# The input of a state-space scan copied to PSUM by ScalarE and multiplied there in place, behind the scan; negated maxima written to PSUM

## The reference

```python
# selective scan, D_INNER = 256 channels, 16 states each
def step(ht, inp):
    x_t, dt_t, B_t, C_t = inp
    dA = jnp.exp(dt_t[..., None] * A)
    dB = dt_t[..., None] * B_t[:, None, :]
    ht = dA * ht + dB * x_t[..., None]
    y_t = jnp.sum(ht * C_t[:, None, :], axis=-1)
    return (ht, y_t)
...
# cross-attention, 16 heads of 8
score = jnp.einsum('bhqd,bhkd->bhqk', qh, kh) / jnp.sqrt(jnp.float32(n_d))
attn = jax.nn.softmax(score, axis=-1)
```

## Time and profile before

| | |
|---|---|
| median of 3 runs | 883.94 us (882.31 to 884.08) |
| span of the profiled execution, which is the only time that the profile gives for it | 889.5 us |
| busy over the span: PE, DVE, ACT, POOL | 81%, 80%, 60%, 72% |
| rounds of the scan | from 27 to 623 us |

### The profile page before, as it was taken

How to read it: one execution, slowest core, us unless ns; L and a number is a source line. 1 busy time by engine, 2 the same in 40 slices (tenths; PEclk the granted TensorE clock), 3 DMA queues, 4 the chain that set the end, 5 groups by cost and what they waited for, 6 DMA issues and landing times. The chain is left out here.

```text
span 889.5 us, 12694 instructions
## 1 busy us (share of the span) xinstructions
PE 721.8 (81%) x3977; PEld 491.0 (55%) x3977; DVE 715.8 (80%) x1060; ACT 531.9 (60%) x1272; POOL 639.2 (72%) x481
## 2 busy tenths in 40 slices
PE   6577578888888889888878888847888998899992
PEld 3343344554445455455535545524565787799982
DVE  4789999999999999999999999999435245455782
ACT  4777569669768877876976795681243342233230
POOL 1278899678989889889998988997422445645552
PEclk9788779999999999899999999987899999999997
DMA  4545575274464646347425533960643346675952
GB/s 99 192 149 146 182 266 192 82 251 145 158 178 155 192 121 203 122 135 211 157 109 184 172 120 107 280 203 25 190 129 105 109 158 196 223 253 168 368 183 76
DMA packets 83917, 148.91 MB, mean 167 GB/s; under 512 B 11201, under 2 KB 56143, under 8 KB 83850
## 3 DMA queue, kind: packets, MB, share of 16 engines
q1 hardware_dynamic: 78858, 139.55, 49.3%
q0 software_dynamic: 4992, 8.54, 2.8%
HBM read 115.34 MB, written 39.27 MB: 174 GB/s over the span
## 5 line engine op out<-in xcount | busy, mean ns | idle before, releaser
L1451 POOL TENSOR_TENSOR prod<-hst,BC 128x1024 f32<-128x1024 f32 x128 | 301.4, 2362 | 62.7 <-DVE hst L1663 49.6
L1663 DVE TENSOR_TENSOR_SCAN hst<-dA,Rp 128x1024 f32<-128x1024 f32 x128 | 292.2, 2283 | 6.4
L1188 ACT ACTIVATE dA<-dtm,Aneg 128x255 f32<-128x255 f32 x512 | 214.8, 496 | 66.0 <-DVE hst L1663 64.1
L1571 POOL DMA_INDIRECT y2d<-prod,back x92 | 91.7, 997 | 125.5 <-DVE prod L1964 103.8
L1456 POOL TENSOR_TENSOR prod<-prod 128x512 f32<-128x512 f32 x128 | 163.6, 1288 | 2.4
L1654 DVE TENSOR_TENSOR Rp<-BC,Rp 128x1024 f32<-128x1024 f32 x128 | 157.0, 1226 | 7.8 <-DMA BC<-bcd 0.6
L638 PE MATMUL Y<-prod,ident 128*128 128x256 f32 x512 | 139.2, 405 | 22.8 <-POOL prod L1456 18.0
L638 PEld LDWEIGHTS Y<-prod,ident 128*128 128x128 f32 x512 | 99.1, 201 | 57.9 <-POOL prod L1456 22.5
L638 PE MATMUL Mb<-hpad,winT 128*128 128x512 f32 (+1 forms) x176 | 82.5, 617 | 15.1 <-ACT xh L1137 13.6
L638 PEld LDWEIGHTS Rp<-BC,xh 128*128 128x128 f32 x736 | 89.1, 192 | 4.8 <-issue 2.6
L638 PE MATMUL Rp<-BC,xh 128*128 128x128 f32 x736 | 89.9, 275 | 0.6 <-DVE prod L1964 0.6
(11 more groups left out here) (254 smaller groups left out, 1215.9 us busy)
## 6 DMA issues: line engine op xcount, KB each, us to landing
BC<-bcd SPq DMA_DIRECT2D x63, 1024.0 KB, 5.4
BC<-recs SPq DMA_DIRECT2D x46, 578.0 KB
xsd<-blank SPq DMA_DIRECT2D x18, 1056.0 KB, 12.4
dtm<-xsd SPq DMA_DIRECT2D x46, 132.0 KB
recs<-in_L_ffn_W SPq DMA_DIRECT2D x16, 256.0 KB
xin<-in_x SPq DMA_DIRECT2D x8, 256.0 KB, 5.8
x2d<-x2o SPq DMA_DIRECT2D x8, 256.0 KB, 5.6
E<-x2d SPq DMA_DIRECT2D x4, 512.0 KB
```

Of the source, the lines that this page charges most:

```text
L1188: m = A(dA[:, k % RING, i, 1:SEQ], dtm[:, r % 2, d, b * SEQ + 1:(b + 1) * SEQ], ACT.Exp, scale=Aneg[:, d, c * NC + i:c * NC + i + 1])
L1451: TT(prod[:, k % RING, :, :], hst[:, k % RING, :, :], BC[:, (k // 2) % BCR, 1, :, :], ALU.mult).then_inc(s_pd, 1)
L1571: pool.indirect_dma_start(out=y2d[:, :], out_offset=bass.IndirectOffsetOnAxis(ap=at, axis=0), in_=yr[:, j % YR, i, :], in_offset=None, bou ...
L1663: v.tensor_tensor_scan(hst[:, k % RING].rearrange("p n s -> p (n s)"), dA[:, k % RING].rearrange("p n s -> p (n s)"), U.rearrange("p n s - ...
```

## The change

ScalarE gets a new function `copy_xh`, which copies `xh` of one sequence into `DTX`; it stands in ScalarE's code behind the decays that it computes in steps 7 and 15, and once ahead of the first decays. `steps_x` waits for that copy and multiplies `DTX` by `dtm` in place, so that one of its inputs is in PSUM. It moves from ahead of the scan of steps 7 and 15 to behind it. The reduction `least` and the product `normed` move with it. `split_max` writes the negated maxima to PSUM (up to round 6; in round 7 to an SBUF tile) and splits them from there, with one instruction more.

```diff
+            def copy_xh(r, b):
+
+                if r or b:
+                    act.wait_ge(s_u, r * STEPS + b * (STEPS // 2))
+                    act.wait_ge(Aa.sem, Aa.at("xh1", r))
+                else:
+                    act.wait_ge(Ha.sem, Ha.at("xh1", 0))
+                A(DTX, xh[:, r % 2, :, b * SEQ:(b + 1) * SEQ], ACT.Copy).then_inc(s_xc, 1)
...
             first_half()
+            copy_xh(0, 0)
...
                 g = r * STEPS + k + 3
                 if g < ROUNDS * STEPS:
                     decays(*divmod(g, STEPS))
+                if k == 7:
+                    copy_xh(r, 1)
+                if k == 15 and r + 1 < ROUNDS:
+                    copy_xh(r + 1, 0)
                 slot(r, k)
...
-                if r or b:
-                    v.wait_ge(s_u, r * STEPS + b * (STEPS // 2))
+                v.wait_ge(s_xc, r * NB + b + 1)
                 half = slice(b * SEQ, (b + 1) * SEQ)
-                v.tensor_tensor(DTX[:, :, :], dtm[:, r % 2, :, half], xh[:, r % 2, :, half], ALU.mult).then_inc(s_dx, 1)
+                v.tensor_tensor(DTX[:, :, :], dtm[:, r % 2, :, half], DTX[:, :, :], ALU.mult).then_inc(s_dx, 1)
...
-                v.tensor_scalar(nm[:, :, 0, 0:HEADS], mx[:, :, :], -1.0, None, ALU.mult).then_inc(Tv.sem, 1)
+                v.tensor_scalar(part, mx[:, :, :], -1.0, None, ALU.mult).then_inc(Tv.sem, 1)
                 v.wait_ge(Tv.sem, Tv.at("ma", r))
-                v.scalar_tensor_tensor(part, mx[:, :, :], -1.0, nm[:, :, 0, 0:HEADS], ALU.mult, ALU.subtract).then_inc(Tv.sem, 1)
+                v.tensor_copy(nm[:, :, 0, 0:HEADS], part).then_inc(Tv.sem, 1)
                 v.wait_ge(Tv.sem, Tv.at("mb", r))
+                v.tensor_tensor(part, part, nm[:, :, 0, 0:HEADS], ALU.subtract).then_inc(Tv.sem, 1)
+                v.wait_ge(Tv.sem, Tv.at("mc", r))
                 v.tensor_copy(nm[:, :, 1, 0:HEADS], part).then_inc(Tv.sem, 1)
-                v.wait_ge(Tv.sem, Tv.at("mc", r))
+                v.wait_ge(Tv.sem, Tv.at("md", r))
                 v.tensor_tensor(nm[:, :, 2, 0:HEADS], part, nm[:, :, 1, 0:HEADS], ALU.subtract).then_inc(Tv.sem, 1)
```

```diff
+                if k == 7:
+                    steps_x(r, 1)
+                    if tail:
+                        least(r - 2)
+                if nxt and k == 15:
+                    steps_x(r + 1, 0)
+                if ln and k == 15:
+                    normed(r + 2)
```

More of the change, by code:

```diff
@@ L301, in decoder @@
         s_bc = [sem(f"s_bc{i}") for i in range(BCR)]
+        s_xc = sem("s_xc")
         s_dx = sem("s_dx")
@@ L313, in decoder @@
         Ta = Marks(sem("Ta"), "KT V sq ln rs q m e00 e01 e10 e11 ld rd x2")
-        Tv = Marks(sem("Tv"), "xq " + " ".join(f"mx{i}a mx{i}b" for i in range(NB * QT)) + " ma mb mc me n")
+        Tv = Marks(sem("Tv"), "xq " + " ".join(f"mx{i}a mx{i}b" for i in range(NB * QT)) + " ma mb mc md me n")
         s_kb = sem("s_kb")
@@ L1772, in middle @@
                         logits(r - 2)
-                    if k == 8:
-                        least(r - 2)
                 if k == 11 and r < ROUNDS:
@@ L1780, in middle @@
                     maxima(r - 1, 2)
[L1781 to L1786, removed]
             def slot(r, k):
```

## The result

The changed kernel takes 932.44 us (927.45 to 933.87, 4 runs) against 883.12 (880.61 to 884.08, 4 runs) of the kernel before on the same chip: a ratio of 1.0523, with a 95% interval of 1.0482 to 1.0563. By the medians it is slower by 49.3 us; 49.0 were forecast. By the ratio, taken at 883.1 us, the loss is 46.2 us (42.6 to 49.7). The kernel before is not steady enough to tell the two apart: beside the first four experiments its median was 886.55 us, and against that the loss would be 45.9.

The account below looks back on a forecast made before the run. VectorE bounds the rounds, the engine that the others wait for. The terms 63.4 - 1.7 - 7.7 - 4.7 give +49.3 us, +49.0 at the median's scale: 883.9 + 49.0 = 932.9, so 933 us; 8 in 10 for 921 to 947.

Parts of the forecast that it names:

- The copy of step 7: Rounds 1 to 7: VectorE's dt*x waits for ScalarE's copy, queued behind slot 6, delaying step 8; +63.4 us together.
- the forecast's 8 to 13 and about 6: Expected VectorE idle time in us ahead of the second dt*x: 8 to 13 in most rounds, about 6 in round 7.
- Step 15: Copy for the first sequence is hidden by the scan; 1.1 us saved at each of 7 places, -7.7 us.
- A cover: At step 15 the copy was to end 0.5 us before the product could start.
- The split: Split of the maxima, 6 rounds: first instruction, from SBUF to PSUM, doesn't wait for GpSimd; 0.78 us each, -4.7 us.
- The waits that go: Attention's norm in rounds 4 and 6 no longer waits 0.87 us for ScalarE's inverse root; -1.7 us.
- the upper ends of its listed terms: Clock +5.4, split +6.3, copy's duration 1, round 6 and step 15's cover +4; given as 928 to 943 us.
- the copy is never late: Rival: ScalarE keeps up at step 7 of every round, only 22.9 us of savings stay, 861 us; 4 in 100.
- The rival of TensorE's clock: Clock falls in more rounds, delaying ScalarE's block; 938 or 952 us; 10 in 100 for above 947.
- rounds 4 and 6 as slow as today: Gate's four matmuls, for which ScalarE's block waits, take 3.78 us in round 4; step 8's delay 11.1 us in both rounds.

Follow-up runs that it names:

- the first four experiments: e1, e2, e3 and e4; the runs of the kernel before beside them had a median of 886.55 us (881.11 to 889.38).
- e1: Changed kernel without ScalarE's copy of step 7, the product there reading xh from SBUF; 869.61 us, ratio 0.9816 to the kernel before.
- e3: Changed kernel with step 7's copy, in rounds 1 to 7, moved into slot 6 ahead of the key blocks; 873.13 us, ratio 0.9846.
- e5: Changed kernel without any copy, both products reading SBUF but still behind the scan, new split kept; 866.13 us, ratio 0.9812.
- e4: Kernel before with only the new split of the maxima added; 881.71 us, ratio 0.9956.
- e2: Changed kernel with ScalarE's copy of step 7 ahead of the decays of step 10 instead of behind; 925.34 us, ratio 1.0445.
- e6: Changed kernel with the first half of the key blocks moved from ScalarE's slot 6 to behind the copy in slot 7; 924.4 us, ratio 1.045.

## Why the prediction was right

**The copy of step 7, forecast +63.4.** The seven distances from the product U of step 7 to that of step 8 (rounds 1 to 7; in round 3 from 277.33, the row below, to 283.11 before, and from 293.95 to 309.02 now) sum to 39.9 us before and 101.5 after: +61.6. The stops read 9.3, 11.1, 10.7, 10.7, 11.5, 11.1 and 6.4 us, within the forecast's 8 to 13 and about 6. e1 and e3 show that the cause is the copy's place behind slot 6: without the copy, or with it ahead of the key blocks, the stop is gone. The copy itself takes 0.58 us of ScalarE (0.63 was taken). At step 15 this costs next to nothing: e1, with the first product's copies, and e5, with none, can't be told apart. At step 7 it isn't free even when in time: in e3 the copy stands ahead of the inverse root in ScalarE's order, and the norm waits for that root 8.2 us within the rounds, against 2.6 in e5.

```profile
277.33 1.23 DVE L1654 TENSOR_TENSOR Rp<-BC,Rp 128x1024 f32<-128x1024 f32 x1
```

**Step 15, forecast -7.7.** The seven distances from the product U of step 15 to the next round's first fell from 41.7 to 33.6 us, and the one of step 7 in round 0 from 5.3 to 4.3: -9.1. A cover was there, but of 0.2 us in round 3 and not of 0.5: the copy was done at 347.45, the product started at 347.67, and ScalarE's decays began 0.19 us ahead of the scan where 0.53 had been read. Too careful was to count nothing for round 6, where the copy was in time. In round 0 the product of step 15 waited 0.96 us, and the place gained 1.2 even so, since dt*x had taken 2.70 there.

**The split, forecast -4.7.** The distance from step 13's U to step 14's fell by 0.8 us in each of rounds 1 to 6, 4.8 together; alone it is worth 3.9 +/- 2.7 (e4). The first instruction's 0.228 us, beside a running product of GpSimd in rounds 1 to 6, agree with the rule on VectorE's single-source operations that the prediction took from the Trainium skill ("SBUF — State Buffer", "Who interferes with whom").

**The waits that go, forecast -1.7.** Only 1.0 went. The attention's norm no longer waits in rounds 4 and 6, but in round 4 the maxima wait 0.86 us for TensorE instead. Nor is it clear that the change took the norm's waits away: in e7, the kernel before once more, they are gone from rounds 4 and 6 too, and one of 0.65 us stands in round 2.

These make 61.6 - 9.1 - 4.8 - 1.0 = +46.7 of the rounds' +50.1. The remaining 3.4 us are 2.2 in the first steps of round 0, where the same kernel varies by 1.4 us between its two profiles, and small waits for TensorE.

So the mechanism and its size were right, and the closeness of the total is luck in part. The terms were off by -1.8, -1.4, -0.1 and +0.7 us, the 3.4 us more were in no term, and by the ratio the loss is 46.2 us, 2.8 below the forecast. The range was also added up loosely: the upper ends of its listed terms sum to 16.7 us, which is 950 and not 943. And it took 0.2% for what a measurement of this kernel can tell, while the kernel's own times range over 1%.

**The rivals.** That the copy is never late ended at 861 in the forecast, by 22.9 us saved. VectorE's busy time in the rounds fell by that, but e3, the version in which the copy is never late at step 7, got 13.6 of it; ScalarE's own lateness met VectorE elsewhere, in the norm's 8.2 us above all. The rival of TensorE's clock happened in a small measure: the granted clock over the rounds fell from 0.92 to 0.88, and in e2 and e6 some 5 us of the shorter stop came back as other waits of VectorE, nearly all for TensorE. But it hardly lengthened ScalarE's block. The gate's four matmuls, in round 5 after the change:

```profile
465.99 2.81 PE L639 MATMUL Mb<-hpad,winT 128*128 128x512 f32 x4 [2.58 <-ACT xh L1138]
```

Of the six rounds whose four matmuls the timeline shows in one piece this is the only one with more than 1.99 us, while before it was 3.78 in two (the earlier trace rows shows one). The forecast had rounds 4 and 6 as slow as today; they were not and lost 3.2 us less than forecast, against 1.5 more in rounds 1 and 5. That is most of the difference between 63.4 and 61.6. By e7 the reading behind the forecast was one of a single execution: the kernel before has these matmuls at 1.98 us in rounds 4 and 6 as well. Why the clock is low in one round and not in another stays open, and so does how much of e2's and e6's missing 4 and 9 us it explains: no run holds the clock fixed, and each of the two is itself uncertain by 5 to 6 us.

**What the prediction missed** is no term of its sum but a reading behind it: it put the 1.1 us of dt*x down to its two SBUF operands alone. They are one condition. The other is the place, ahead of the scan, where GpSimd's product was running in 14 of the 16 instances, and e5 shows that moving the product behind the scan takes the price from 1.820 to 0.767 us without any copy. The prediction had the place in its working, since the change moves it, but gave it no price of its own and no rival.

## What to carry to other kernels

Before an operation is given to an idle-looking engine, look where in that engine's own order it will stand and what lies ahead of it, not at its busy share: ScalarE was 60% busy over the span and yet some 10 us late at this one place, and its lateness had been free because a ring of four buffers stood between it and VectorE. The copy has no such ring: it can be made only when the product U has read `DTX`, and it is wanted one scan later. And where two engines block each other, first try to move the short operation to a time when the other is done; here that, with the new split, gained 16.6 us (e5), no less than any version with a copy.

## What the runs showed of the hardware

- A VectorE product with two SBUF operands (128x512) waits for GpSimd's running product or addition to end: in round 3 before, it began at 278.66, GpSimd's product ended at 280.23 and VectorE's at 280.79. If it is first, GpSimd waits: in e5 a GpSimd operation of 0.25 us took 0.67 when it began 0.11 us behind VectorE's. With one operand in PSUM the product took 0.67 to 0.70 us in all 16 places of the changed kernel, of which eight had a GpSimd operation running at the product's start, and 0.67 beside GpSimd's product in round 1 of e3. The Trainium skill, "SBUF — State Buffer", "Who interferes with whom", says so of two SBUF inputs, and that the order of issue decides who blocks; the traces agree on both.
- A copy of 128x512 f32 by ScalarE from SBUF to PSUM takes 0.58 us, and VectorE's waiting product starts 0.10 us after it.
- The same four matmuls of 128x512 took 1.98 us in rounds 4 and 6 of one execution of the kernel before and 3.78 in another. The granted clock over 16 us of round 4 was 1.00 in the first, which is the 2.4 GHz level throughout, and 0.79 in the other, a mix of the two levels.
- The end of one and the same kernel, behind its last scan, lasted 266.9 us in one execution and 256.3 in another, and its times went from 880.6 to 889.4 us.
